# A decoder layer of 16 tiles: the applying step of its layer norms on GpSimd, new orders on every engine, and waits left out

## What is computed

```python
def _layernorm(x, axis=-1, eps=1e-05):
    m = jnp.mean(x, axis=axis, keepdims=True)
    v = jnp.var(x, axis=axis, keepdims=True)
    return (x - m) / jnp.sqrt(v + eps)
...
x = _layernorm(x + _L0_attn_ref(x, ...))           # min-GRU, 16-head causal attention, gated FFN
x = _layernorm(x + _L0_xattn_ref(x, ctx, ctx, mask, ...))
x = _layernorm(x + _L0_ffn_ref(x, Wr, Wi, Wo))     # 8 experts, best 2 of each row
```

## Time and profile before

| | before |
|---|---|
| median of 3 runs | 231.37 us (230.54 to 232.62) |
| the profiled execution | 233.95 us |
| its span, first to last instruction | 232.2 us |
| PE busy | 212.8 us, 92% |
| PEld busy | 176.3 us, 76% |
| DVE busy | 186.9 us, 81% |
| ACT busy | 172.1 us, 74% |
| POOL busy | 141.2 us, 61% |
| mean granted clock of PE | 0.975 |

### The profile page before, as it was taken

How to read it: one execution, slowest core, us unless ns; L and a number is a source line. 1 busy time by engine, 2 the same in 40 slices (tenths; PEclk the granted TensorE clock), 3 DMA queues, 4 the chain that set the end, 5 groups by cost and what they waited for, 6 DMA issues and landing times. The chain is left out here.

```text
span 232.2 us, 7656 instructions
## 1 busy us (share of the span) xinstructions
PE 212.8 (92%) x2168; PEld 176.3 (76%) x2168; DVE 186.9 (81%) x667; ACT 172.1 (74%) x663; POOL 141.2 (61%) x302
## 2 busy tenths in 40 slices
PE   7789499999999999999999999999999999997940
PEld 3678498889897979887897898888979867975310
DVE  3658277677887978899698999988789977999785
ACT  4899679997788788887588867887867687673450
POOL 5457526666668474677467586764674776564552
PEclk9999979999999999999999999999999999999795
DMA  4986653545244234324024352434141000000000
GB/s 105 255 250 164 147 134 93 145 124 156 57 96 104 54 95 101 106 49 102 5 49 106 73 144 74 108 92 108 47 128 47 28 13 6 11 14 14 11 23 23
DMA packets 33720, 20.09 MB, mean 87 GB/s; under 512 B 20496, under 2 KB 31248, under 8 KB 33680
## 3 DMA queue, kind: packets, MB, share of 16 engines
q1 hardware_dynamic: 32992, 19.35, 32.2%
q10 hardware_dynamic: 688, 0.26, 0.4%
HBM read 14.16 MB, written 5.24 MB: 84 GB/s over the span
## 5 line engine op out<-in xcount | busy, mean ns | idle before, releaser
L2402 DVE TENSOR_REDUCE neg_max<-ps 128x4 f32<-128x512 f32 x64 | 43.0, 676 | 7.1 <-PE ps L902 6.8
L464 POOL TENSOR_TENSOR rs<-ss,neghalf 128x1 f32<-128x1 f32 x48 | 28.4, 595 | 25.6 <-ACT junk L1628 25.3
L1715 ACT ACTIVATE probs<-ps 128x512 f32<-128x512 f32 x64 | 38.5, 605 | 4.7 <-PE ps L922 4.5
L464 POOL TENSOR_TENSOR lrs<-mv,neghalf 128x1 f32<-128x1 f32 x48 | 26.3, 552 | 21.8 <-DVE mv L2493 8.7
L1052 PE MATMUL ps<-w_moe,y2T 128*128 128x512 f32 x64 | 34.0, 621 | 0.0
L969 PE MATMUL ps<-xT,guT 128*128 128x128 f32 x256 | 33.2, 276 | 0.0
L969 PEld LDWEIGHTS ps<-xT,guT 128*128 128x128 f32 x256 | 30.9, 192 | 1.3 <-ACT xT L1744 1.0
L525 POOL TENSOR_SCALAR_AFFINE_SELECT probs<-probs 128x600 f32<-128x600 f32 x32 | 24.4, 761 | 8.8 <-ACT probs L1715 8.5
L900 PE MATMUL ps<-k_stack,q_stack 125*128 125x128 bf16 x256 | 25.3, 222 | 2.8 <-DMA k_stack<-qk_scratch 2.8
L922 PE MATMUL ps<-q_stack,k_stack 128*128 128x128 bf16 x256 | 24.8, 219 | 0.0
L900 PEld LDWEIGHTS ps<-k_stack,q_stack 125*128 125x128 bf16 x256 | 18.5, 100 | 5.5 <-issue 4.0
(11 more groups left out here) (156 smaller groups left out, 588.1 us busy)
## 6 DMA issues: line engine op xcount, KB each, us to landing
q_stack<-qk_scratch SPq DMA_DIRECT2D x48, 96.0 KB
k_stack<-qk_scratch SPq DMA_DIRECT2D x48, 96.0 KB
qk_scratch<-qk_parts SPq DMA_DIRECT2D x16, 192.0 KB, 2.2
ctx_sb<-in_ctx_dram SPq DMA_DIRECT2D x4, 256.0 KB, 4.3
qk_scratch<-qk_parts SPq DMA_DIRECT2D x16, 64.0 KB, 2.0
out_dram<-x_all SPq DMA_DIRECT2D x16, 64.0 KB, 1.5
x_all<-in_x_dram SPq DMA_DIRECT2D x2, 256.0 KB, 3.1
raw<-in_L_ffn_Wi_dram SPq DMA_DIRECT2D x1, 512.0 KB, 6.3
```

The source lines that it names most:

```text
L464: nc.gpsimd.tensor_tensor(dst, src, neghalf[:], ALU.pow).then_inc(S[rsd], 1)
L1715: nc.scalar.activation(probs[:, b, n, :, :], view("probs", 4 * k + n), ACT.Exp, scale=HD ** -0.5).then_inc(S["att_p"], 1)
L2402: nc.vector.tensor_reduce(neg_max[:, b, QUARTER * n:QUARTER * n + QUARTER], view("scores", 4 * k + n), AX_X, ALU.max, negate=True).then_in ...
```

## The change

**The apply.** `layernorm_apply` and its three callers go from DVE's list to POOL's, always somewhere behind the power of the same tile and norm. The instruction stays the same, with the same operands.

**Waits.** Waits that follow from others are left out: on all engines steps no longer wait for the readers of tile k - 2, where an order or another wait already implies it, and so on. `power`, for one, loses its second wait; so do about 50 further steps on DVE, ACT, POOL and PE. No wait is added but that of the moved apply.

**SP's list.** Wout and the small tensors leave the first group of loads; context tiles 4 to 7 are loaded there instead. Wout is loaded between the first save and the first stack, the small tensors after the third `max_stack`, the context tiles 8 to 15 behind the second and third save.

**Orders and banks.** The lists of PE, DVE, ACT and POOL and the table `HOME` are new throughout. PE has 14 filler matmuls, where it had 10.

```diff
-WEIGHTS = ("w_gru", "w_qkv", "w_ox", "w_kq", "w_gate", "w_up", "w_ei", "w_ej", "w_m0", "w_m1", "w_out")
+WEIGHTS = ("w_gru", "w_ox", "w_kq", "w_qkv", "w_ej", "w_ei", "w_gate", "w_m1", "w_up", "w_m0", "w_out")
...
-            load_out()
-            load_small()
+            load_ctx(1)
             load_x(3)
             parts_save(0)
-            load_ctx(1)
+            load_out()
             parts_stack(0)
             parts_save(1)
+            load_ctx(2)
             parts_stack(1)
             parts_save(2)
+            load_ctx(3)
             max_stack(0)
...
-            def power(src, dst, ready, k, rsd, used):
-
-                after_all(pool, (ready, k + 1), (used, k - 1))
+            def power(src, dst, ready, k, rsd):
+
+                after(pool, ready, k + 1)
                 nc.gpsimd.tensor_tensor(dst, src, neghalf[:], ALU.pow).then_inc(S[rsd], 1)
...
+            def layernorm_apply(n, k, b, src, dst, rsd, done):
+                after(pool, rsd, k + 1)
+                nc.gpsimd.tensor_scalar(dst, src, mv[:, n, b, 0:1], lrs[:, n, b:b + 1], ALU.subtract, ALU.mult).then_inc(S[done], 1)
...
-            def layernorm_apply(n, k, b, src, dst, rsd, done):
-                after(dve, rsd, k + 1)
-                nc.vector.tensor_scalar(dst, src, mv[:, n, b, 0:1], lrs[:, n, b:b + 1], ALU.subtract, ALU.mult).then_inc(S[done], 1)
...
             def moe_mix(k):
...
-                after(dve, "moe_c", k + 1)
-                after(dve, "moe_z", k - 1)
```

More of the change, by code:

```diff
@@ L30 @@
 HOME = {
[L31 to L68, removed]
+    "w_gru": "2",
+    "gru_turn": "4636343237677575",
+    "gru_gates": "0204601637141206",
+    "w_ox": "5",
+    "ctx_turn": "6216073740502610",
+    "w_kq": "4",
+    "gru_turn_back": "1221540230766036",
@@ new lines @@
+    "w_qkv": "3",
+    "ctx_project": "5514563511612317",
+    "qkv_turn": "4707323644334414",
+    "qk_project": "7556763631427516",
+    "w_ej": "0",
+    "v_project": "2204527306323052",
+    "w_ei": "7",
+    "w_gate": "0",
+    "w_m1": "3",
+    "w_up": "2",
+    "w_m0": "7",
+    "w_out": "6",
+    "scores": "4101745136717171304434142046411505002640510643764025754153704311",
+    "max_turn": "2600113117511404",
+    "probs": "2712006607136663050716520515406156050004666554433260252736713062",
@@ L1086, in _ @@
-            gru_gates(4)
-            w_ej()
-            w_m0()
-            ctx_project(2)
-            gru_gates(5)
-            gru_turn(6)
-            gru_turn_back(3)
-            w_m1()
-            ctx_turn(4)
-            ctx_project(3)
+            gru_turn(3)
+            w_ej()
+            gru_turn(4)
+            ctx_project(1)
+            ctx_turn(3)
+            v_project(0)
+            gru_gates(3)
+            w_ei()
+            w_gate()
+            ctx_project(2)
+            w_m1()
@@ L1096, in _ @@
+            qkv_turn(1)
+            w_up()
+            ctx_turn(4)
+            gru_turn(5)
+            gru_gates(4)
+            ctx_turn(5)
+            qk_project(1)
+            gru_turn_back(2)
+            gru_turn(6)
+            ctx_project(3)
+            gru_gates(5)
+            ctx_project(4)
+            gru_turn_back(3)
+            gru_turn(7)
+            ctx_project(5)
+            w_m0()
+            qkv_turn(2)
             gru_turn_back(4)
             gru_gates(6)
-            qkv_turn(2)
+            ctx_turn(6)
@@ new lines, in _ @@
+            qk_project(9)
+            scores_turned(7, 2)
+            moe_turn(3)
+            ffn_gate(5)
+            moe_logits(3)
+            att_values(6)
+            scores_turned(7, 3)
+            xat_turn_probs(4)
+            moe_experts(3, 0)
+            v_project(8)
+            xat_values(4)
+            att_back(6)
+            att_values(7)
+            ctx_turn(14)
+            att_turn(6)
+            moe_experts(3, 1)
+            att_project(6)
+            ffn_down(5)
+            gru_turn(14)
@@ L1310, in _ @@
+            moe_turn(4)
+            qkv_turn(10)
+            att_back(7)
+            scores(8, 0)
+            v_project(9)
+            moe_logits(4)
+            scores(8, 1)
+            att_turn(7)
+            moe_experts(4, 0)
+            xat_turn(5)
+            att_project(7)
+            gru_gates(13)
+            xat_scores(5)
+            qkv_turn(11)
             scores(8, 2)
-            ctx_project(9)
+            qk_project(10)
+            moe_experts(4, 1)
+            xat_turn_probs(5)
@@ L1387, in _ @@
[L1387 to L1405 removed]
+            ctx_project(14)
@@ new lines, in _ @@
+            ffn_turn(6)
+            qk_project(11)
+            ctx_turn(15)
+            ffn_turn(7)
+            xat_values(5)
+            ffn_gate(6)
+            gru_gates(14)
+            ctx_project(15)
+            max_turn(8)
+            scores(9, 0)
+            ffn_up(6)
+            moe_turn(5)
+            ffn_gate(7)
+            ffn_up(7)
+            moe_logits(5)
+            scores_turned(8, 0)
+            gru_turn_back(13)
+            ffn_down(6)
+            scores_turned(8, 1)
@@ new lines, in _ @@
+            gru_turn(15)
+            moe_experts(5, 0)
+            scores_turned(8, 2)
+            scores(9, 1)
+            gru_turn_back(14)
+            scores_turned(8, 3)
+            scores(9, 2)
+            ffn_down(7)
+            scores(9, 3)
+            moe_experts(5, 1)
+            qkv_turn(12)
+            att_values(8)
+            scores(10, 0)
+            v_project(10)
+            max_turn(9)
+            att_back(8)
+            xat_turn(6)
+            gru_gates(15)
+            xat_scores(6)
```

2543 lines of the change are left out of this document (1213 added, 1330 removed).

## The result

The changed kernel takes 237.99 us (237.40 to 238.55, 4 runs) where the kernel before takes 231.8 in the same comparison: 1.026 of it, 95% interval 1.022 to 1.031. It is slower by 6 us; I had forecast 3.8 us faster. Its profiled execution has a span of 235.6 us.

What follows compares the result with a forecast made beforehand. PE was taken to bound the kernel from 50 to 210 us, leaving gains only at start and end. Start 2.4, end 1.4, middle and waits 0: 3.8 us off the 231.37 median, 227.6 us, range 224.0 to 232.0.

Steps and rivals of the forecast that it cites:

- The price of the apply: All 48 applies moved from DVE to POOL: 0.35 us each assumed, from a tensor_scalar with constants at 0.31.
- The upper bound of 0.73: Most that an apply on POOL was taken to cost, from an add of two tensors of twice the size.
- The middle at 0: From 50 to 210 us, where PE is full: no gain; from 1.1 us gained to 3 lost if POOL delivers y later.
- GpSimd is late: Rival: 32 applies that feed PE transposes each come 0.3 us late on POOL, 9.6 us in all, 237 us; chance 0.11.
- The left-out waits at 0: Waits dropped on DVE, ACT, POOL and PE: costed at 0, up to 0.3 us on the last chain.
- The start: 0 to 50 us: 2.4 us gained (0 to 3.6) from more PE work before tile 0's first scores and half the clock dip.
- the first rival: Start gives nothing: the hole may belong to the profiled execution, and ACT is full there; 230.0 us, chance 0.24.
- the hole: PE's idle 2.79 us before tile 0's first scores at 28.59, waiting for k_stack's DMA; 1.9 us of new PE work fits in.
- the clock dip: PE at 0.50 clock from 29.4 to 32.8 us, behind the hole, 1.7 us lost; half of it, 0.85, counted as gained.
- about even: Start, SP queue: loads exchanged ahead of the save and between save and stack balance, so the stack lands no later.
- The end: From 210 us: 1.9 us gained on DVE around tile 15, less 0.5, so 1.4 us; from 0.5 lost to 3.6 gained.
- where I charged 0.5: End: moe_add(12) on POOL between tile 15's first power and its apply, costing between 0 and 1.1 us, taken as 0.5.

Runs made afterwards that it cites:

- madd_const: The changed kernel with its GpSimd apply multiplying by and adding constants instead of subtracting and multiplying by two columns (layer norms left out of the result): 228.38 us, 0.983.
- lean_again: The kernel before with only the implied waits left out (32 on ACT stay), measured a second time with more executions: 231.01 us, 0.990 of the kernel before.
- lean_before: The kernel before with only the implied waits left out (32 on ACT stay), first measurement: 230.76 us, 0.992 of the kernel before.
- loads_old: The changed kernel with add-and-multiply apply and a DVE sign step (1.012), but first loads in the order of before: 237.05 us, 1.027 of the kernel before.
- tail_swap: The changed kernel with one pair of POOL calls exchanged, ffn_layernorm(15) ahead of moe_add(12): 239.48 us, 1.033 of the kernel before.

## Why the prediction was wrong

**The price of the apply** is the step that failed. "I take 0.35 us, since form and size are those of the first and only the two column operands are new": the form was not the same. gru_a multiplies and adds; the apply subtracts and multiplies, and that pair costs 0.65 with constants, 0.80 with columns. The upper bound of 0.73, from the largest row that I showed, was too low as well, so the whole range stood on a price that the operation never had. madd_const has that price, and the forecast's time with it: 0.983 of the kernel before, against 227.6 / 231.4 = 0.984. Between it and the changed kernel, alike but for the form of the apply, lie 4.4%, some 10 us.

The Trainium skill ("GPSIMD Engine Reference", section 4.1 Engine selection) had warned: put elementwise work on VectorE. Its figure of about 2x for two inputs came out near: 0.80 against 0.43 and 0.36 on DVE. The runs bear out the advice for this form, but not number of inputs as its reason: the same three operands take 0.45 us when the first operation is an add.

**The middle at 0** failed by that price. POOL at 178 us is 76% of the span, which sounded harmless as a mean, but the work comes in stretches where it is all wanted at once (18.82 of 20 us from 190 to 210). The rival "GpSimd is late" was the case that came. That its 237 us lie near 238.0 is luck: it wanted 9.6 us from 32 late y, and PE waits 3.2 us for y in all, 1.4 of it in the middle. The waits in the middle (50 to 210 us), the first two rows from the changed kernel, the last from madd_const:

```profile
PE ps L906 <- POOL y L492: 1.4, 5, 0.4
PE ps L961 <- DMA k_stack<-qk_scratch: 1.3, 4, 0.5
...
PE ps L961 <- DMA k_stack<-qk_scratch: 1.8, 4, 0.9
```

The rest of the 5.1 us are 0.8 for xn, whose power rs stood behind an output apply (198.36 in the chain above), 1.1 for the gate, nearly all at 108.82 us, where DVE had waited for an output apply ahead of it, and short pieces. The wait for k_stack is not the price: it stands at 0.31 too, and the kernel before has none in this stretch, so it came with the new orders, which I had put at 0 here.

Idle time shows half of the price. From 50 us to the down projection of tile 15 PE does 1749 matmuls in the changed kernel (first row) as in madd_const:

```profile
50.00:212.70 162.70, 157.36 (x1749) 131.50 (x1748) 130.64 (x472) 119.20 (x449) 134.23 (x262) 1.00 0.27 69
...
50.00:206.00 156.00, 154.01 (x1749) 131.71 (x1748) 128.18 (x467) 118.52 (x447) 115.83 (x263) 1.00 0.28 72
```

That is 6.70 us more, 3.35 of them idle and 3.35 busy. The busy half would be matmuls that come one by one and overlap less; that is my reading and not shown.

**The left-out waits at 0** was wrong too, in the other direction: 2 to 2.8 us in the changed kernel, some tenths to 1% in the kernel before. The row that I read the earlier trace rows gives a wait of 0.02 us, and the moe_mix group shows that DVE hides them. Neither was POOL: there an apply loses 0.10 us to two further waits, and 130 went. Which engine gains in the kernel before stays open.

**The start**, 2.4 us: PE's part came as described, the loads did not. The save is issued at 18.19 us (18.5 forecast), but the stack at 20.58, 2.4 us behind it and 2.4 us sooner than in the kernel before, where 6.7 us lay between them. I had called the loads between them even. So the first scores of tile 0 find their stack there, and PE is at work right before them, at full clock:

```profile
20.58 0.38 SPq L343 DMA_DIRECT2D q_stack<-qk_scratch  x1
...
27.85 0.38 PE L961 MATMUL ps<-k_stack,q_stack 125*128 125x128 bf16 x4
```

How much of it lasts can't be read from the changed kernel. From 40 to 50 us PE is busy 8.72 of 10, waiting 1.1 for ACT's probs, where before it had 9.45:

```profile
40.00:50.00 10.00, 9.45 (x124) 8.48 (x122) 6.94 (x18) 9.44 (x36) 5.85 (x16) 1.00 0.59 142
```

ACT is full there in both (9.57 and 9.44), so part goes back, as the first rival had it. That rival has another point: the hole isn't the same in every execution. In the profiled one of lean_again, which keeps the old orders, the clock dip is missing too:

```profile
0.00:50.00 50.00, 43.83 (x416) 36.56 (x417) 32.21 (x85) 43.92 (x183) 29.25 (x70) 1.00 0.66 167
```

PE is busy 43.8 us there, against 42.4 and 45.1, and waits 1.5 us at the hole; in the profiled execution of lean_before, the same kernel, it waits 2.4 and is busy 42.8, with the dip (0.97). So a part of my 2.4 us was one execution's, how large a part I can't say. loads_old shows that PE's new order needs the new load order, worth 3.5 us; "about even" hid that, because I weighed the loads for the stack and not for the context that PE now wants sooner.

**The end**, 1.4 us: from the down projection of tile 15 (212.70 us) to the end of the span there are 22.9 us, as before (209.27 to 232.2). With the apply at 0.31 it is 20.6 us, to a span of 226.6. The rows of before and of madd_const:

```profile
209.27 1.16 PE L991 MATMUL ps<-outT,hidden 128*128 128x128 f32 x8
...
206.00 1.09 PE L1051 MATMUL ps<-outT,hidden 128*128 128x128 f32 x8
```

So in these executions the end was worth 2.3 us at the price assumed, and nothing at 0.80. Part of that is the granted clock: 0.73 from 220 to 225 us in the changed kernel, 1.00 in madd_const until PE has nothing left, at 220 us. moe_add(12) costs 1.25 us between power and apply, PE waits 1.31, where I charged 0.5; tail_swap shows that it can't simply be moved.

The forecast also rested on sums that balanced, and that was luck: with the price right, some 2 us of the gain would be the waits that I put at 0, so start, end and middle together would bring nearer 2 than 3.8 us. That split is a difference between runs, with the waits measured at the price of 0.80, and not measured by itself.

## What to carry to other kernels

Price a moved instruction by a row on the new engine with the same operations in the same places, and not by one of the same shape: here add with multiply and subtract with multiply of the same tile lay 0.35 us apart. Where no such row exists, the far bound is a case of its own: work out what the engine's fullest stretch looks like at that price before giving it a small chance. A wait that has come true is not free everywhere: put back on POOL alone, such waits made the changed kernel 1.9 us slower by the medians, so count them on an engine that is full for a stretch.

## What the runs showed of the hardware

On GpSimd a tensor_scalar of 128x128 with one operation and one column takes 0.61 us, more than multiply and add together with two columns (0.47), so leaving an operation out made it slower.

A sum of two tensors on DVE takes much longer beside some of POOL's instructions than beside others. In the changed kernel's last stretch:

```profile
218.20 0.72 POOL L551 TENSOR_TENSOR term_pairs<-terms 128x256 f32<-128x256 f32 x1
218.27 0.80 DVE L2557 TENSOR_TENSOR z<-acc 128x128 f32<-128x128 f32 x1
...
230.88 0.80 POOL L492 TENSOR_SCALAR x_all<-z,mv,lrs 128x128 f32<-128x128 f32 x1
231.26 0.29 DVE L2557 TENSOR_TENSOR z<-acc 128x128 f32<-128x128 f32 x1
```

The sum takes 0.80 us beside POOL's add of two tensors and 0.29 where it lies wholly inside the apply. On the mean it went from 0.33 us in the kernel before to 0.46, 2.0 us for 16, a part of why DVE's total fell to 174.3 us and not to the 167 that I expected. The Trainium skill ("SBUF — State Buffer", section "SBUF: two separate sides") tells of a port pair that a DVE instruction with two inputs in SBUF, as this sum has, and a GpSimd instruction hold in turn, each to its end; the first pair of rows agrees with it, the second, beside the apply, shows no blocking.
